# Which expert does a block use: two packed words with shifts and masks, or one load into eleven registers

## The reference

```python
logits = x @ gate_w.T                                  # 16 experts
rw, sel = jax.lax.top_k(softmax(logits), 2)            # two experts per row
gu = jnp.einsum('nd,edf->nef', x, w_gate_up)
g, h = jnp.split(gu, 2, axis=-1)
h = silu(g) * h
expert_out = jnp.einsum('nef,efd,ne->nd', h, w_down, combine)
out = expert_out + shared                              # a gated ffn that all rows pass
```

## Time and profile before

| | |
|---|---|
| median of 3 runs | 1146.05 us (1142.23 to 1146.54) |
| profiled execution, its own time | 1145.96 us |
| its span in the trace | 1144.2 us |
| PE / PEld / DVE / ACT / POOL busy | 85 / 74 / 70 / 50 / 43% |
| `experts`, about 640 to 893 us | PE busy 220.9 us of 253 |

### The profile page before, as it was taken

One profiled execution on the slowest core, in us unless ns is written; L12 is line 12 of the kernel. 1 busy time (PEld: TensorE's weight loads), 2 busy tenths in 40 slices (PEclk: granted clock), 3 DMA queues, 4 the chain that ended last, 5 costly groups with the idle time before them and its releaser, 6 DMA issues. The chain is left out here.

```text
span 1144.2 us, 28387 instructions
## 1 busy us (share of the span) xinstructions
PE 969.2 (85%) x9192; PEld 844.1 (74%) x9193; DVE 800.4 (70%) x2071; ACT 574.1 (50%) x1309; POOL 490.3 (43%) x726
## 2 busy tenths in 40 slices
PE   5997998998899407999999589998999799888972
PEld 4776887776788405888888588888888687777761
DVE  5887997787998693544444267777777377776855
ACT  5993446996345313444444345554555344444442
POOL 4322556220555334767776100000000557877874
PEclk9998998998999557999999799999999899999995
DMA  4333688432678527566654445555544536665553
GB/s 134 112 98 88 179 248 261 140 115 58 171 204 248 186 99 240 179 199 221 217 188 167 120 143 161 159 162 159 158 152 155 146 123 196 193 191 172 162 164 110
DMA packets 188966, 188.16 MB, mean 164 GB/s; under 512 B 55120, under 2 KB 169936, under 8 KB 188752
## 3 DMA queue, kind: packets, MB, share of 16 engines
q1 hardware_dynamic: 173088, 149.25, 43.0%
q0 software_dynamic: 12288, 33.57, 8.8%
q10 hardware_dynamic: 3504, 4.20, 1.1%
HBM read 100.81 MB, written 86.14 MB: 163 GB/s over the span
## 5 line engine op out<-in xcount | busy, mean ns | idle before, releaser
L994 POOL DMA_INDIRECT sorted_rows<-yr,sl x128 | 138.3, 1080 | 77.5 <-issue 38.0
L1283 POOL DMA_INDIRECT cy<-expert_rows,csl x128 | 139.4, 1089 | 45.2 <-issue 44.0
L607 PE MATMUL bank<-xbd,am 128*32 128x68 f32 x4096 | 138.1, 304 | 10.9 <-DMA xbd<-xn_scratch 5.7
L607 PEld LDWEIGHTS bank<-xbd,am 128*32 128x32 f32 x4096 | 122.7, 128 | 18.4 <-issue 9.8
L1276 POOL MEMSET czero<- 128x4 f32 x1 | 0.1, 101 | 260.1 <-POOLq L1059 260.1
L1156 PE MATMUL bank<-eh,xh 128*128 x288 | 95.5, 332 | 0.6 <-DVE xl L1200 0.6
L896 DVE TENSOR_TENSOR s_hf<-s_sg,bank 128x512 f32<-128x512 f32 (+1 forms) x48 | 33.0, 688 | 89.3 <-ACT s_sg L871 89.3
L1200 DVE TENSOR_TENSOR xl<-bank,xh 128x256 fp32r<-128x256 f32 x144 | 61.2, 425 | 42.9 <-ACT xh L1182 41.9
L1182 ACT ACTIVATE xh<-bank 128x256 fp32r<-128x256 f32 x144 | 55.5, 385 | 69.2 <-PE bank L1129 69.0
L1129 PE MATMUL bank<-ident,xg 128*128 128x128 f32 x288 | 57.1, 281 | 34.0 <-issue 23.1
L408 DVE TENSOR_TENSOR am<-probs,mask 128x512 f32<-128x512 f32 x128 | 80.0, 688 | 8.4 <-ACT probs L502 7.5
(11 more groups left out here) (199 smaller groups left out, 3146.4 us busy)
## 6 DMA issues: line engine op xcount, KB each, us to landing
xg<-sorted_rows SPq DMA_DIRECT2D x144, 128.0 KB, 2.1
expert_rows<-yo SPq DMA_DIRECT2D x144, 128.0 KB, 1.8
xbd<-xn_scratch SPq DMA_DIRECT2D x128, 72.0 KB, 2.3
xt<-x SPq DMA_DIRECT2D x32, 256.0 KB, 3.0
xn_scratch<-xn SPq DMA_DIRECT2D x64, 128.0 KB, 2.8
xr<-x SPq DMA_DIRECT2D x32, 256.0 KB, 3.6
x_scratch<-x SPq DMA_DIRECT2D x32, 256.0 KB, 3.5
yn_scratch<-yn SPq DMA_DIRECT2D x32, 256.0 KB, 3.5
```

What stands on the lines that cost most here:

```text
L607: ins = nc.tensor.matmul(pso[q][t][J * b:J * b + J, g * MW:(g + 1) * MW], am[:, q, g, e, side], xbd[:, q, e + side, :, g], start=(g == 0 a ...
L994: nc.gpsimd.indirect_dma_start(out=xg_d, out_offset=bass.IndirectOffsetOnAxis(ap=sl[:, q, t, u, k:k + 1], axis=0), in_=yr[:, t, u], in_off ...
L1283: nc.gpsimd.indirect_dma_start(out=y[:, v, k, j], out_offset=None, in_=yg_d, in_offset=bass.IndirectOffsetOnAxis(ap=sl[:, v, k, j:j + 1], ...
```

## The change

`routing` no longer packs: VectorE copies `pb[4]` straight into the integer tile `block_expert`, one expert number per entry. At the start of a turn TensorE's sequencer fetches eleven entries (R + 3) in one call, with no check of bounds, and each step takes its register as it is, with no shift and no mask.

```diff
-        block_expert = sb("block_expert", [1, NBLK + 1 + PACK], I32)
+        block_expert = sb("block_expert", [1, NBLK + 1 + 12], I32)
...
-            done(v.memset(bexp[:, NBK:], 0.0))
+            done(v.memset(block_expert[:, NBK:], 0))
...
-            done(v.tensor_copy(bexp[:, 0:NBK], pb[4][0:1, 0:NBK]))
-            src = bexp
-            for k in range(1, PACK):
-                done(v.scalar_tensor_tensor(packed[:], bexp[:, k:k + NBK + PACK], float(1 << (PACK_BITS * k)),
-                                            src[:, 0:NBK + PACK], ALU.mult, ALU.add))
-                src = packed
-            done(v.tensor_copy(block_expert[:], packed[:]))
+            done(v.tensor_copy(block_expert[:, 0:NBK], pb[4][0:1, 0:NBK]))
...
-            held, words = {}, []
-
-            def load_words(b):
-                words.clear()
-                for k in range(2):
-                    at = block_expert[0:1, bass.ds(b + PACK * k, 1)]
-                    w = pe.value_load(at, min_val=0, max_val=(1 << (PACK_BITS * PACK)) - 1)
-                    words.extend((w, PACK_BITS * j) for j in range(PACK))
+            held, loaded = {}, []
+
+            def load_experts(b):
+                loaded[:] = nc.values_load_multi_w_load_instructions(
+                    block_expert[0:1, bass.ds(b, R + 3)], engines=(mybir.EngineType.PE,), min_val=0, max_val=E - 1,
+                    skip_runtime_bounds_check_because="routing clamps every block's expert to 0 .. E - 1")[1]
 
             def find(_, r):
-                if words:
-                    w, shift = words.pop(0)
-                    held[r] = (w >> shift) & (E - 1)
+                if loaded:
+                    held[r] = loaded.pop(0)
 
             def enter(n, r):
-                load_words(n - 1)
+                load_experts(n - 1)
                 for k in range(-1, 2):
                     find(n + k, (r + k) % R)
...
-            load_words(0)
+            load_experts(0)
```

More of the change, by code:

```diff
@@ L41 @@
 SPARE = NBLK + 1 + E
-PACK, PACK_BITS = 5, 4
 EPS = 1e-5
@@ L685, in routing @@
         s_clear = sem("r_clear")
-        bexp = sb("bexp", [1, NBK + 2 * PACK])
-        packed = sb("packed", [1, NBK + PACK])
         gh, gl, dh, dl = split
```

## The result

The kernel after takes 1139.72 us (median of 5 runs, 1137.78 to 1142.32), the kernel before 1144.87 us (median of 5 in the same comparison). The ratio is 0.9946, with a 95% interval of 0.9924 to 0.9968: faster by about 5 us where 22.8 were forecast. The profiled execution took 1137.78 us.

The account below looks back on a forecast made before the run. PE was taken as TensorE-bound within a turn of `experts` and sequencer-bound at its seam. Seams 13.3, shifts and masks 7.6, behind the loop 0.3 and packing 1.6 summed to 22.8 us off 1145.96: 1123.2 us, range 1116 to 1153.

Parts of the forecast that it names:

- The seam: Between turns of `experts`, one load replaces two checked loads: saves 1.34 - t, 18 times, 13.3 us in all.
- t: Length of the seam's new eleven-register load, taken as 0.6 us between bounds of 0.30 and 2.6.
- my upper bound: Seam load with a separate memory trip of 0.23 us for each of ten further registers: t = 2.6 us.
- Shifts and masks: Sequencer operations in the steps of `experts`; removal saves 0.45 us a turn, 7.6 us over 17 turns.
- The three longer steps: Later steps of a turn where shift and mask follow the wait for `xl`; 0.07 to 0.09 us each, 0.24 saved.
- The first step's 0.21: First step of a turn, where the sequencer has no lead; removing shifts and masks saves 0.21 us.
- Routing's 1.6 us: VectorE's packing tail at the end of `routing`, alone holding the barrier; removing it saves 1.6 us.
- The load ahead of the first step: Before the expert loop, a load of up to 1.9 us is hidden by the DMA of `xg`; costed at nothing.
- Behind the loop: Steps after the expert loop, without shifts and masks, save perhaps 0.3 us.
- the second, in pieces: Rival: the seam's call becomes a few loads, t = 1.1 us, 13.8 us saved, 1132 us; chance 0.10, shared with t up to 1.55.
- The first rival, register by register: Seam load makes one trip per register, t = 2.6 us, 13.9 us slower, 1160 us; chance 0.19.
- break-even of 1.87 us: Seam load length t at which the register-by-register rival turns, 0.157 us per further register.

Follow-up runs that it names:

- experiment 5: Kernel after with entries stored doubled and a shift and mask put back before each use; ratio to before 1.0034, turn 13.63 us.
- experiment 7: Kernel before with four aligned packed words per load, unchecked, shifts and masks kept, gate_up products reordered so only the last two wait for `xl`; ratio to before 0.9815.
- experiment 10: Kernel after with unawaited TensorE semaphore increments: eight or thirty-two ahead of the pipeline, or four per turn; profiled 1143.33, 1135.49 and 1150.01 us.
- experiment 9: Kernel after unaltered again, ratio to before 0.9941; and kernel after with unused packing put back, `routing` 40.88 us instead of 39.15.
- experiment 1: Kernel after with eighteen extra loads of 1 to 14 registers ahead of the expert stage; eleven took 1.32 us, no kernel time given.
- Experiment 2: Kernel after with 28 extra loads of varied first entry, count and step; twelve registers begun one entry off took 2.88 us, no kernel time given.

## Why the prediction was off

**The seam: the step that failed is t.** "I take 0.03 us for each further register" had no row of a load behind it, only the length of a plain register operation. Measured, a further trip is 0.23 to 0.24 us, the very figure of my upper bound, and a trip brings either one register or four aligned ones. That makes 1.32 us for eleven by themselves and 1.51 in the loop. With t = 1.51 the term 18 x (1.34 - t) is -3.1 instead of +13.3 us. The measured seam is 0.08 us better than that (0.09 longer, not 0.17), which makes -1.6. (The prediction speaks of eight records that leave the seam; its rows have seven, with seven gaps up to L1127's, and their sum, 0.99 us, is right.)

**Shifts and masks.** The three longer steps went from 1.48 to 1.40 as forecast, 0.24 us a turn, and experiments 5 and 7 show the mechanism, with both of its parts. The first step's 0.21 came as 0.06. Moved by thirty-two instructions it comes as 0.16 (1.58 to 1.43): the term was 0.05 too high, and 0.10 us went into the hole of experiment 10, which the first step of before doesn't have. A turn so won 0.30 in the steps instead of 0.45, 5.1 us instead of 7.6.

**Routing and the rest.** Routing's 1.6 us came (40.75 to 39.13) and went again with the packing (experiment 9), so VectorE alone holds that barrier. The load ahead of the first step was hidden by `xg`, as forecast. Behind the loop 0.4 us came (10.57 to 10.15 from its first transpose to the last product).

**The sum again.** -1.6 + 5.1 + 0.4 + 1.6 = 5.5 us; measured are 5.15 between medians. Of the 17.3 us missing, 14.9 are the seam's term, and 2.5 the first step's; 0.1 more than forecast came behind the loop. The saving at the seam, more than half of the forecast, was never there; what remained came from the two smaller terms.

**The rivals.** Nearest was the second, in pieces: the call does go in pieces of up to four registers, but inside one instruction, and with an unaligned or incomplete piece broken into single trips. I had priced eleven registers at three pieces, 1.1 us; they are five. The first rival, register by register at 2.6 us, is what the same instruction would have done from an entry not divisible by four (2.88 us for twelve). Its break-even of 1.87 us is consistent with the result, since 1.51 was still a small gain; no run came near it. The bounds from below and above, 0.30 and 2.6, held too; choosing a point near the lower end on the length of an ALU_OP was the mistake, when the only row of a load said that the trip is the price.

Rows 4 had 0.30 us for one register, and experiment 1 has 0.31. The Trainium skill, "DMA: Bandwidth & Descriptors", section "Latency and other measured facts", gives a floor of some 600 ns. Here the floor is half of that. Experiment 2 gives 0.24 us a register for an unaligned load of twelve and 0.07 for an aligned one. The Trainium skill, "Runtime: NRT & Kernel Launch", section "Instruction fetch mechanics", has about 200 ns a register even for bulk, for loads from HBM; the trace agrees for unaligned words and not for aligned groups of four.

## What to carry to other kernels

A load into several registers is priced by its trips: begin at an entry divisible by four (16 bytes on in the tile; where the tile itself lies was not varied), fetch multiples of four even if some are not needed, and leave no remainder (five cost 0.61 us, eight 0.59). Put such loads where the sequencer is ahead of its engine, not between two turns of a loop, where each of its operations shows (the two checks of bounds alone took 0.38 us of this gap). And where two bounds lie a factor of nine apart and one of them is built from the only row of the thing itself, weigh that row first.

## What the runs showed that was not expected

- One load takes 0.31, 0.54, 0.77 and 0.34 us for one to four registers, 0.84 for twelve and 1.10 for sixteen, aligned.
- The load of eleven takes 1.32 us ahead of the pipeline and 1.44 to 1.56 in most turns. The medians of aligned loads of four and twelve show no such difference (0.33 and 0.34, 0.85 and 0.84), though six of the nineteen loads of twelve took 0.90 to 1.07. Why is open.
- A hole of some 0.15 us stays at one place among TensorE's instructions while they are moved past it; moved by thirty-two, it is no longer in the first step, and a turn is 0.10 to 0.14 us shorter (12.87 against 12.97 and 13.01). A comparison of two versions of such a loop can be off by this much for no other reason than where the instructions lie.
- Semaphore increments that nothing waits for, at the top of a turn, cost 0.5 us for four (13.53 against 13.01).
